# A fused attention and feed-forward kernel: its last feed-forward product as three rounded ones, GpSimd computing the low parts, in a rearranged tail

## The reference, cut to what matters

```
x = x + cross_attention_0(layernorm(x), ctx, ...)        # 16 heads
x = x + fp8_ffn(layernorm(x), w_fc, w_proj)              # operands rounded to e4m3, relu squared
x = x + softmax(scores(ctx) * layernorm(x) + masks)      # "qc_score" is the gate of the scores
# the last layer, on h0 = layernorm(x):
v   = rmsnorm(h0, norm1_w) @ wv + bv
h   = h0 + v @ wo
mlp = (silu(rmsnorm(h, norm2_w) @ w_gate) * (rmsnorm(h, norm2_w) @ w_up)) @ w_down      # 256 -> 704 -> 256
x   = x + where(sigmoid(h0 . w_router + b_router) > 0.5, h + mlp, h0)
```

## Time and profile before

| | us |
|---|---|
| median of 3 runs | 431.35 (431.34 to 431.42) |
| the profiled execution, its time | 430.39 |
| its span, first to last instruction | 428.6 |
| TensorE busy, with 2028 products | 397.7 (93%) |
| VectorE busy | 299.7 (70%) |
| ScalarE busy | 200.8 (47%) |
| GpSimd busy | 185.6 (43%) |
| mean granted TensorE clock | 0.984 of full speed |

### The profile page before, as it was taken

The page is one execution under the profiler, slowest core; times in us unless marked ns, Lnnn a source line. Parts: engine busy times, 40 slices in busy tenths (PEclk is TensorE's granted clock), DMA queues, the critical chain, the costliest instruction groups (busy, mean ns, idle before and its releaser), DMA issues.

```text
span 428.6 us, 6012 instructions
## 1 busy us (share of the span) xinstructions
PE 397.7 (93%) x2028; PEld 247.6 (58%) x2033; DVE 299.7 (70%) x673; ACT 200.8 (47%) x550; POOL 185.6 (43%) x172
## 2 busy tenths in 40 slices
PE   8799899999999999999999999889687788999997
PEld 8665556666666566566555777544143354544574
DVE  5796698757676767676687656568899997735432
ACT  1523655565555555565547763266893025231100
POOL 2545455655565556545655123758501340450000
PEclk9999999999999999999999999996899899999999
DMA  7635020020020300000300004100000000000011
GB/s 255 212 136 203 1 98 2 2 98 2 8 92 2 99 1 1 2 0 8 130 0 2 0 0 114 63 2 0 1 0 2 0 2 1 0 0 2 12 37 49
DMA packets 9086, 17.51 MB, mean 41 GB/s; under 512 B 2145, under 2 KB 6945, under 8 KB 8161
## 3 DMA queue, kind: packets, MB, share of 16 engines
q1 hardware_dynamic: 9056, 17.14, 11.9%
HBM read 16.09 MB, written 1.05 MB: 40 GB/s over the span
## 4 chain that ended last, share of the span: by engine, by line
PE 63%; DVE 23%; ACT 8%; issue 4%; DMA 2%; SPq 0%; DVEq 0%; ACTq 0%
PE bank L1255 7%; PE bank L1479 6%; PE bank L1249 6%; PE bank L1224 6%; PE bank L1495 6%; PE bank L1131 5%; PE bank L1237 5%; PE bank L1133 4%; PE bank L1132 4%; DVE rot_up L774 3%; PE bank L1209 3%; ACT prob L581 3%; PE bank L1154 3%; DVE tail_all L1037 2%; ACT probT L572 2%
## 5 line engine op out<-in xcount | busy, mean ns | idle before, releaser
L415 POOL TENSOR_TENSOR prob<-prob,rinv 128x512 f32<-128x512 f32 x64 | 66.6, 1041 | 106.3 <-DVE rinv L832 106.3
L581 ACT ACTIVATE prob<-bank,negmax 128x256 f32<-128x256 f32 x128 | 60.1, 479 | 40.6 <-DVE negmax L827 40.6
L827 DVE TENSOR_REDUCE negmax<-bank 128x2 f32<-128x512 f32 x64 | 41.3, 687 | 25.1 <-PE bank L1224 24.7
L572 ACT COPY probT<-bank 128x512 f32<-128x512 f32 x64 | 37.9, 592 | 19.7 <-PE bank L1237 19.5
L410 POOL TENSOR_TENSOR rot_low<-rot_low,rot_up 128x512 f32<-128x512 f32 x32 | 40.9, 1277 | 11.2 <-DVE rot_up L774 11.2
L774 DVE TENSOR_TENSOR rot_up<-bank,cb 64x512 f32<-64x512 f32 x64 | 44.1, 689 | 0.9
L1131 PE MATMUL bank<-xnT,w 128*128 128x512 f32 x96 | 42.0, 437 | 2.2 <-DVE xnT L750 1.7
L1237 PEld LDWEIGHTS bank<-ca,prob 128*128 128x128 f32 x256 | 30.5, 141 | 18.9 <-issue 16.1
L1237 PE MATMUL bank<-ca,prob 128*128 128x128 f32 x256 | 38.9, 275 | 1.8 <-ACT probT L572 1.1
L1479 PE MATMUL bank<-tailT,blobs 128*128 128x512 f32 (+1 forms) x96 | 38.9, 596 | 1.6 <-ACT tailT L522 1.6
L772 DVE TENSOR_TENSOR rot_low<-bank,cb 128x512 f32<-128x512 f32 x32 | 22.1, 689 | 25.6 <-PE bank L1133 25.5
(11 more groups left out here) (197 smaller groups left out, 708.6 us busy)
## 6 DMA issues: line engine op xcount, KB each, us to landing
blobs<-in_blob SPq DMA_DIRECT2D x7, 1024.0 KB, 4.9
xs<-in_x SPq DMA_DIRECT2D x2, 512.0 KB, 4.1
xn<-in_w_fc_t SPq DMA_DIRECT2D x1, 1024.0 KB, 4.8
ctxT<-in_w_proj_t SPq DMA_DIRECT2D x1, 1024.0 KB, 5.5
out<-qk SPq DMA_DIRECT2D x8, 128.0 KB, 1.7
cb<-in_const_b SPq DMA_DIRECT2D x1, 768.0 KB, 8.6
blobs<-in_w_gate SPq DMA_DIRECT2D x1, 704.0 KB, 4.2
blobs<-in_w_up SPq DMA_DIRECT2D x1, 704.0 KB, 5.6
```

The lines of the kernel that those rows point to most:

```text
L415: pool.tensor_tensor(p[:], p[:], rinv[:, n % PROBS, :].unsqueeze(2).to_broadcast([P, 2, S]), ALU.mult).then_inc(normed, 1)
L572: act.copy(probT[n % 2][:].rearrange("p a s -> p (a s)"), pT[:]).then_inc(probsT_copied, 1)
L581: ins = act.activation(prob[n % PROBS][:, st, :], pS[n % 2][:, st * S:(st + 1) * S], ACT.Exp, bias=negmax[:, n % 2, st:st + 1], accum_out= ...
```

## The change

Nothing up to the end of the attention loop changes but the places of some arrays in memory. In the tail:

- The down product becomes three float32r products. ScalarE rounds w_down (`wd_high`) and each gated slice (`gated_hi`) to float32r; VectorE subtracts to get `wd_rest`, GpSimd to get `gated_lo` (`low_part`).
- Half 0's four down tiles are computed between gate_up(5) and gate_up(6), the others at the end. Two tiles at a time leave their last slice of 64 rows for the end (`down_two`). Their results are added in two groups too; the base sum is split in two.
- The gate and up steps start with three bank pairs, then use two. turn_norm(1) moves from step 3 to step 4, attend(1) behind step 4.
- norm_tiles(0) goes from VectorE to ScalarE; x2_tile, h_tile, h8 and the tasks of half 1 are put in another order on VectorE.
- In the front, the scores go behind the expansions, with fillers in their old place; the first xn tile goes from GpSimd to VectorE; turn_largest is issued ahead of value_out.

The diff, cut to its core:

```diff
-QK_BANK = (0, 2, 1, 3)
+QK_BANK = (0, 2, 4, 5)
+GATE_PAIR = (0, 1, 2, 0, 1, 0, 1, 0, 1, 0, 1, 0)
+GATED_FIRST = (0, 0, 0, 1, 2, 4, 5, 6, 7, 8, 9, 10)
+DOWN_BANK = (4, 5, 0, 1, 4, 5, 6, 7)
...
+        wd_high = sb("wd_high", [P, FT1, D], F32R)
+        wd_rest = sb("wd_rest", [P, FT1, D], F32R)
+        gated_hi = sb("gated_hi", [P, FT1, CH], F32R)
+        gated_lo = sb("gated_lo", [P, FT1, CH], F32R)
...
 # GpSimd
-            for t in range(NT):
+            for t in range(1, NT):
                 pool.tensor_scalar(xn[:, t, :], xs[:, t, :], negmean[:, t:t + 1], xscale[:, t:t + 1],
...
+            def low_part(n):
+                c, ft = n // FT1, n % FT1
+                m = rows_of(ft)
+                pool.wait_ge(gated_high, n + 1)
+                pool.tensor_tensor(gated_lo[0:m, ft, :], gatedT(ft, c * CH, CH), gated_hi[0:m, ft, :].bitcast(F32),
+                                   ALU.subtract).then_inc(gated_low, 1)
+            for n in range(3):
+                low_part(n)
             powers(11, 1, c_ve, c_y)
+            for n in range(3, FT1):
+                low_part(n)
             pool.wait_ge(norm_ready, 2 * NT)
             pool.wait_ge(h2_ready, NT)
-            pool.tensor_tensor(qk1[:], xs[:], xn[:], ALU.add).then_inc(base_ready, 1)
+            for gr in range(2):
+                lo, hi = gr * NT // 2, (gr + 1) * NT // 2
+                pool.tensor_tensor(qk1[:, lo:hi, :], xs[:, lo:hi, :], xn[:, lo:hi, :], ALU.add).then_inc(base_ready, 1)
+            for n in range(FT1, 2 * FT1):
+                low_part(n)
...
 # ScalarE: qk_copy(0), (1) go ahead of tile 6 of the steps, then
+            qk_copy(2)
+            qk_copy(3)
+            act.wait_ge(d_ffn1, 64)
+            for p, k in wd_parts:
+                act.copy(wd_high[p, k, :], wd[p, k, :]).then_inc(wd_rounded, 1)
             softmax(0)
+            act.wait_ge(shift3_ready, 1)
+            for t in range(4):
+                act.activation(xn[:, t, :], xs[:, t, :], ACT.Identity, bias=negmean[:, t:t + 1],
+                               scale=rstd[:, t:t + 1]).then_inc(norm_ready, 1)
...
+            def high_part(n):
+                c, ft = n // FT1, n % FT1
+                act.wait_ge(act_ready, n + 1)
+                if c:
+                    act.wait_ge(down_ready, 4)
+                act.copy(gated_hi[0:rows_of(ft), ft, :], gatedT(ft, c * CH, CH)).then_inc(gated_high, 1)
+            silus(0); silus(1); high_part(0); silus(2); high_part(1); silus(3)
+            turned_copy(8, tailT, turned_copied, (2, 3))
+            high_part(2); high_part(3); silus(4); h_squares(1); high_part(4); silus(5); high_part(5)
+            turned_copy(10, tailT, turned_copied, (2, 3))
+            silus(6); silus(7); high_part(6); silus(8); high_part(7); silus(9); high_part(8)
+            silus(10); high_part(9); high_part(10); silus(11); high_part(11)
...
 # VectorE
+            dve.wait_ge(inv_ready, 1)
+            dve.tensor_scalar(xn[:, 0, :], xs[:, 0, :], negmean[:, 0:1], xscale[:, 0:1],
+                              ALU.add, ALU.mult).then_inc(v_first, 1)
...
             h8_tile(5)
-            x2_tile(4)
             x3_sums(0)
             x3_statistics(0)
+            x2_tile(4)
+            newton(5, rstd, 0, half)
+            dve.scalar_tensor_tensor(out=negmean[:, 0:half], in0=mv[:, 0:half, 0], scalar=-1.0, in1=rstd[:, 0:half],
+                                     op0=ALU.mult, op1=ALU.mult).then_inc(shift3_ready, 1)
             h8_tile(6)
             x2_tile(5)
-            norm_tiles(0)
-            h8_tile(7)
+            newton(6, r1, 0, half, of=(c_q, c_y1))
+            h_tile(0)
+            h8_first(7)
+            for t in range(1, half):
+                h_tile(t)
+            h8_second(7)
             x2_tile(6)
-            h_tiles(0)
-            ins = x2_tile(7)
             h_square(0)
-            in_order(ins)
+            newton(7, r2, 0, half)
+            h2_tiles(0)
+            in_order(x2_tile(7))
             aggregate(8, half, NT)
             gate_scores(1)
-            h2_tiles(0)
             mask_scores(1)
             largest(1)
+            dve.wait_ge(wd_rounded, 2)
+            for p, k in wd_parts:
+                dve.tensor_tensor(wd_rest[p, k, :], wd[p, k, :], wd_high[p, k, :].bitcast(F32),
+                                  ALU.subtract).then_inc(wd_low, 1)
             x3_sums(1)
...
 # VectorE, gated products (result(t) adds and selects a tile)
+            gated(0); x3_statistics(1); gated(1); norm_tiles(1); newton(10, ...); gated(2); gated(3); h_tile(4)
+            gated(4); h_tile(5..7); h_square(1); gated(5); newton(11, ...); h2_tiles(1); add_base(0..3); routes()
+            result(0..3); gated(6); gated(7); gated(8); add_base(4..7); gated(9); gated(10); gated(11); result(4..7)
...
 # TensorE
+            turn_largest(1)
+            value_out(0)
             largest_everywhere(1, 2)
+            value_out(1)
...
-            qk_scores(0) ... qk_scores(3), between turn_x8(0) and expand(0)
+            keep_busy(8, 6)
+            turn_x8(0)
+            for t in range(1, 4):
+                keep_busy(2, 6)
+                turn_x8(t)
...
+            turn_largest(2)
+            qk_scores(0)
             largest_everywhere(2, 4)
+            for b in range(1, B):
+                qk_scores(b)
...
-            keep_busy(32, 3)
+            keep_busy(28, 3)
             contract(5)
-            keep_busy(16, 3)
+            keep_busy(24, 3)
+            pe.wait_ge(qk_copied, 8)
+            turn_norm(0)
             contract(6)
-            keep_busy(4, 3)
-            turn_norm(0)
             attend(0)
             contract(7)
...
+            def down(t, fts):
+                for ft in fts:
+                    m = rows_of(ft)
+                    pe.wait_ge(gated_low, FT1 * (t // 4) + ft + 1)
+                    ins = product(down_bank(t)[:, 0:D], (gated_hi[0:m, ft, (t % 4) * P:(t % 4 + 1) * P],
+                                                         gated_lo[0:m, ft, (t % 4) * P:(t % 4 + 1) * P]),
+                                  (wd_high[0:m, ft, :], wd_rest[0:m, ft, :]), ft == 0, ft == FT1 - 1)
+                return ins
+            def down_two(t):
+                down(t, range(FT1 - 1))
+                down(t + 1, range(FT1 - 1))
+                for i in range(2):
+                    down(t + i, (FT1 - 1,)).then_inc(down_ready, 1)
+            for n in range(5):
+                gate_up(n)
+            pe.wait_ge(act_ready, 3)
+            attend(1)
+            gate_up(5)
+            pe.wait_ge(wd_low, 2)
+            pe.wait_ge(h_ready, 6)
+            down_two(0)
+            turn(2, atbuf, h2_ready, 0, (2, 3))
+            for t in (2, 3):
+                down(t, range(FT1)).then_inc(down_ready, 1)
+            pe.wait_ge(turned_copied, 12)
+            for n in range(6, 2 * FT1):
+                gate_up(n)
+            down_two(4)
+            for t in (6, 7):
+                down(t, range(FT1)).then_inc(down_ready, 1)
```

More of the change, by code:

```diff
@@ L173, in part @@
                 return loop_only.enter_context(nc.sbuf_tensor(name, shape, dt))
+            kva = part("kva", [P, NT, DC], F32)
+            wkvo = part("wkvo", [P, PAIRS, D], F32)
+            prob += [part(f"prob_{i}", [P, 2, S], F32) for i in range(1, PROBS)]
+            probT = [part(f"probT_{i}", [P, 2, S], F32) for i in range(2)]
             xnT = [part(f"xnT{i}", [P, DK, TOK]) for i in range(2)]
@@ L692, in _, with silus @@
             softmax(1)
-            for n in range(2 * FT1):
-                m = min(P, FF1 - n % FT1 * P)
+            def silus(n):
+                m = rows_of(n % FT1)
                 act.wait_ge(gate_ready, n + 1)
@@ L1002, in norm_tiles, with h_tile @@
                     normalise(t).then_inc(norm_ready, 1)
[L1004 to L1012, removed]
+            def h_tile(t):
+                dve.wait_ge(res_ready, t + 1)
+                dve.wait_ge(shifted_ready, t + 1)
+                dve.scalar_tensor_tensor(out=hbuf(t), in0=res_bank(t)[:, 0:D], scalar=r1[:, t:t + 1],
+                                         in1=atbuf(t), op0=ALU.mult, op1=ALU.add).then_inc(h_ready, 1)
             def h_square(gr):
@@ L1110, in _, with result @@
+            def result(t):
                 dve.wait_ge(down_ready, t + 1)
                 dve.wait_ge(base_added, t + 1)
-                in_order(dve.tensor_tensor(hbuf(t), bank[4 + t % 4][:, 0:D], hbuf(t), ALU.add))
+                dve.tensor_tensor(hbuf(t), down_bank(t)[:, 0:D], hbuf(t), ALU.add).then_inc(down_taken, 1)
+                dve.wait_ge(down_taken, t + 1)
+                dve.wait_ge(base_ready, t // half + 1)
                 dve.copy_predicated(qk1[:, t, :], routed[:, t:t + 1].to_broadcast([P, D]), hbuf(t))\
@@ L1114, in _ @@
                     .then_inc(y_ready, 1)
+            gated(0)
+            x3_statistics(1)
+            gated(1)
+            norm_tiles(1)
+            dve.wait_ge(variance_ready, 10)
```

(29 more changed lines are left out.)

189 lines of the change are left out of this document (96 added, 93 removed).

## The result

The changed kernel takes 427.56 us (median of six runs, 426.48 to 428.92) against 431.35 us (430.58 to 432.1) beside it: ratio 0.9918 [0.9892, 0.9943], 3.8 us faster where 7.5 were forecast. It lies in the range, and the gain is half of the forecast. The profiled execution took 426.81 us, its span is 424.9 us.

A forecast was written before the change was run, and what follows sets the result against it. The tail was taken as bound by VectorE from 331.96 to 356.53, then by TensorE. Terms -4.3+0.9-2.9-1.2 = -7.5 us brought 431.35 to 423.9 us, range 421.0 to 428.5.

The forecast's parts named there:

- Products: Down products: 144 f32r records at 0.12 us plus six row changes, 19.6 us against 23.9, so -4.3 us.
- excursion to 64 rows: Down tiles: the step from 128 to 64 rows and back, six at 0.39 us, 2.3 us in all.
- rival (d): All 144 down products: f32r weight loads not covered at 256 columns, spacing 0.217 us, total 436.3 us; chance 0.10.
- gate_up(0): Start of the gate and up steps: 4.1 us earlier than 356.53, from the front's -1.2 and VectorE's stretch's -2.9.
- -1.2: The front, 276.58 to 304: scores behind the expansions and earlier xscale, 1.2 us less, bounds 0 and -1.85.
- -2.9: VectorE's stretch, 331.96 to 356.53: h2_tiles(0) ends at 352.0, gate_up(0) at 353.6; -2.9 us, bounds -1 and -3.7.
- the better bound: The front: with 16 fillers more TensorE may hold 2.4 GHz, giving -1.85 us rather than -1.2.
- h8(6): VectorE's stretch: GpSimd's bias tiles slow this step, charged at 0.9 us.
- Rival (c): The front gives nothing and VectorE's stretch only 1 us: 427.0 us; chance 0.10.
- Waits from gate_up(0) on: Gate, up and down stage: new waits of 2.0 us against 1.1 before, so +0.9 us.
- The stalls on low parts: TensorE waiting for GpSimd's low parts: about 1.6 us in the first half, 0.2 in the second.
- Rival (b): GpSimd ends last: VectorE's work slows the low parts to 2.0 us each, total 427.4 us; chance 0.12.

The follow-up runs named there:

- (8): Scaling of the gate and up weights moved from GpSimd to ScalarE behind softmax(0), against the changed kernel: 426.18 us, ratio 0.9864.
- Experiments 1 to 4: Each against the changed kernel: newton(10) behind gated(3), 425.5 us; freeing additions ahead of routes(), 424.87; base sum sliced, 425.76; low parts sliced, 421.32.
- (7): GpSimd's low part replaced by gated_hi times a constant, TensorE taking the high part instead, against the changed kernel: one run, span 426.4 us.
- newton_late: VectorE's newton(10) moved from ahead of gated(2) to behind gated(3), against the changed kernel: 425.5 us, ratio 0.9879.

## Why the prediction was right in part and wrong in part

- **Products, -4.3 forecast, -3.6 measured.** The mechanism was right, with a spacing of 0.119 us where 0.12 was taken. Less its stalls the first half's pair takes 5.19 us (378.26 to 384.60), its single tiles 5.04, the second half 10.08: 20.3 in all, against 19.6. The excursion to 64 rows was counted six times at 0.39; a new start behind each stall costs 0.1 more. That weight loads are covered at equal rows held at 256 columns too; rival (d) fell with that.
- **gate_up(0), -4.1 forecast (-1.2 and -2.9), -4.28 measured.** Right in the sum, not in its parts. The first h8 step comes at 307.57, only 0.6 us earlier: the clock held at 1.00 over the expansions, as the better bound had it, but the chain to the scale lost 1.0 to GpSimd's scaling (8), which before had run beside it without holding its lines. From there on 3.7 us are won rather than 2.9. h8(6) lost 0.41 (1.63 for 1.22), not 0.9, but two lines of newton(6) took 0.52 and 0.65, which I had not charged; why the stretch won more than forecast in spite of them I did not test. Rival (c), a front that gives nothing and only 1 us from VectorE's stretch, fell with the 4.28.
- **Waits from gate_up(0) on, +0.9 forecast, +3.8 measured.** This step failed. "All 12 copies and 12 subtractions lie beside products of 3.4 us, except around two points" looked at TensorE alone as who could be hurt. The stalls on low parts were forecast as 1.6 + 0.2 and came as 1.15 + 0.31. The holes of 1.97 and 1.50 had no term: VectorE's durations had been taken over unchanged, with GpSimd now at work beside them. Experiments 1 to 4 show as their cause that GpSimd holds VectorE's lines. The other 0.4 us by which the stage grew (69.60 for 69.04, while these two terms make +0.2) stand in no term of mine.
- **Rival (b)** had the right pair of engines, and its 427.4 is nearly the result, but that is luck: GpSimd's low parts stayed at 1.26 to 1.30 us; VectorE was the victim. The rows to see it were on the table: beside the bias tiles an h8 step took 1.74 us for 1.22, and I charged that once, to h8, as a slowdown in proportion, not to every small line as a wait for the end of an instruction. The same bias tiles already held two of the four norm tiles (0.81 us for 0.41 each, inside the 2.19 of the earlier trace rows). "In the loop 1.28 held beside a VectorE that was busy too" was no evidence: there VectorE mostly reads PSUM, and where it does not, at 234.76, a 128x512 SCALAR_TENSOR_TENSOR took 1.35 us for 0.68.

## What to carry to other kernels

When work is put on GpSimd, list what VectorE does meanwhile and mark its TENSOR_TENSOR, SCALAR_TENSOR_TENSOR and TENSOR_SCALAR instructions whose operands are all in SBUF: beside a GpSimd instruction with two SBUF operands of 256 columns or more, such a line took as long as that one had still to run, however small it was, so a chain of tiny dependent operations is the worst neighbour. Put such chains, and anything that TensorE waits for, elsewhere, or give the work to VectorE itself, where a low part cost 0.68 us and held nobody. And price a rewrite of the products apart from the reordering that comes with it: here the reordering alone brought 3 us more than the two together.

## What the runs showed of the hardware

- A 4-element VectorE operation took 0.16 us alone and up to 1.22 beside GpSimd; a 256-column one 0.41 and 2.61. As a rule one got through for each GpSimd instruction; in the run of (7) one addition at 384.92 was held over both halves of the base sum, 5.19 us.
- Not held: lines beside GpSimd's 128x4 power (newton(5), 0.14 to 0.17 us each), and BATCH_NORM_STATS2 of 256 columns beside a bias tile (0.43 us).
- With one operand GpSimd let go after 0.63 of 1.48 us (512 columns). The scaling (704 columns, 2.03 us each) held single VectorE lines by 0.4 to 0.6 us, to 0.83 to 0.87 us after its start.
- The change from 128 to 64 rows and back costs a down tile about 0.4 us; a second one in the same tile brought it from 2.50 to 2.9.
- f32r products of 256 columns follow at 0.119 us with a fresh 128x128 load each, and at 0.21 us at the 1.2 GHz level (newton_late, near 382).
